# Top-2 expert layers: the inner rows made in turned form, with stationary weights that VectorE picks

## The reference, cut to what matters

```python
# third layer (x: 6250 x 256, layer-normalised first)
logits = xf @ gate_w + gate_b
probs = softmax(logits); top2_vals, top2_idx = top_k(probs, 2)
h = gelu(xf @ w1 + bb1)          # exact gelu, for each expert
y = h @ w2 + bb2
out = sum over the two chosen experts of weight * y
# fourth layer: the same, with a weight of 1 for each of the two
```

## Time and profile before

| | us |
|---|---|
| median of 3 runs (8054.05 to 8055.25) | 8055.03 |
| profiled execution: span from first to last instruction | 9107.5 |
| profiled execution: what lies around the span | not listed |
| expert stage of the third layer: first matmul to first second-layer matmul | 12.15 |
| the same stage: from there to the end of the last second-layer matmul | 424.46 |
| expert stage of the fourth layer, same two parts | 12.02, 424.12 |

### The profile page before, as it was taken

How to read it: one execution, slowest core, us unless ns; L and a number is a source line. 1 busy time by engine, 2 the same in 40 slices (tenths; PEclk the granted TensorE clock), 3 DMA queues, 4 the chain that set the end, 5 groups by cost and what they waited for, 6 DMA issues and landing times. The chain is left out here.

```text
span 9107.5 us, 91729 instructions
## 1 busy us (share of the span) xinstructions
PE 5351.0 (59%) x20514; PEld 4012.4 (44%) x20515; DVE 3669.3 (40%) x8808; ACT 3376.1 (37%) x8020; POOL 4734.0 (52%) x4927
## 2 busy tenths in 40 slices
PE   3789555555534444789433335456556466566796
PEld 2656333444423333656433333344445344445564
DVE  7544555555710000544300001455455455455644
ACT  2522233333333333445333333233334233333553
POOL 5113455555466666034366664666564666664143
PEclk8689776777767776789555555677677767777698
DMA  1421333333233333211201111333332333332213
GB/s 56 178 74 61 91 92 91 86 88 91 67 94 92 92 91 92 84 54 63 79 22 23 23 23 32 94 88 92 87 91 71 95 93 91 88 88 77 94 63 124
DMA packets 395135, 723.41 MB, mean 79 GB/s; under 512 B 117204, under 2 KB 252470, under 8 KB 391602
## 3 DMA queue, kind: packets, MB, share of 16 engines
q0 software_dynamic: 210544, 509.17, 20.1%
q1 hardware_dynamic: 177622, 201.65, 6.9%
q10 hardware_dynamic: 6508, 8.01, 0.2%
HBM read 600.76 MB, written 123.53 MB: 80 GB/s over the span
## 5 line engine op out<-in xcount | busy, mean ns | idle before, releaser
L952 POOL DMA_INDIRECT g_rows<-table,src_idx x2352 | 2244.2, 954 | 1407.4 <-issue 669.9
L1227 PE MATMUL g_p_win<-g_rows,g_hot 128*128 128x264 f32 (+1 forms) x4704 | 1555.7, 490 | 42.5 <-issue 36.0
L1227 PEld LDWEIGHTS g_p_win<-g_rows,g_hot 128*128 128x128 f32 x4704 | 1105.9, 246 | 309.8 <-issue 72.3
L1117 ACT ACTIVATE g_hot<-iota,near 128x128 f32<-128x128 f32 x2352 | 721.4, 387 | 1199.0 <-DMA r_gb<-in_L_ffn_gate_b_dram 873.0
L952 POOL DMA_INDIRECT g2p_rows<-rows,src_idx x784 | 749.3, 956 | 370.4 <-issue 227.7
L952 POOL DMA_INDIRECT gcnp_rows<-table,src_idx x784 | 748.2, 954 | 368.6 <-issue 228.8
L1033 DVE TENSOR_TENSOR g_rows<-g_rows,g_p_w 128x1792 f32<-128x1792 f32 x336 | 679.0, 2021 | 51.1 <-issue 21.2
L1241 PE MATMUL g_p_f<-ones 1*128 1x4 f32 (+1 forms) x336 | 85.9, 324 | 863.9 <-issue 414.1
L1189 PE MATMUL gcnp_p_out<-gcnp_win,gcnp_moved 128*128 128x64 f32 x224 | 62.0, 432 | 732.4 <-ACT gcnp_win L1151 629.7
L1040 DVE TENSOR_TENSOR agg<-agg,g2p_p_out 128x256 f32 x112 | 42.1, 418 | 1102.6 <-PE g2p_p_out L1189 454.1
L1241 PEld LDWEIGHTS g_p_f<-ones 1*128 1x128 f32 x336 | 72.0, 265 | 931.5 <-issue 931.5
(11 more groups left out here) (832 smaller groups left out, 11533.3 us busy)
## 6 DMA issues: line engine op xcount, KB each, us to landing
g_rows<-table,src_idx POOLq DMA_INDIRECT x2352
back<-agg SPq DMA_DIRECT2D x7, 1792.0 KB, 35.0
g_inj<-inject SPq DMA_DIRECT2D x56, 224.0 KB
g2p_rows<-rows,src_idx POOLq DMA_INDIRECT x784
rows<-r_row SPq DMA_DIRECT2D x98, 128.0 KB
gcn_row_in<-back SPq DMA_DIRECT2D x14, 896.0 KB
gcnp_rows<-table,src_idx POOLq DMA_INDIRECT x784
c_row<-back SPq DMA_DIRECT2D x14, 896.0 KB, 13.3
```

The costliest lines, as they stand in the source:

```text
L952: gp.indirect_dma_start(rows[:, s, j, 0:width + H], None, table, bass.IndirectOffsetOnAxis(g.src_idx[:, at:at + 1], 0)).then_inc(got[s], 16)
L1117: last = nc.scalar.activation(hot[:, j, :], g.iota[:, :], ACT.Square, scale=-1.0, bias=g.near[:, bass.ds(c * J + j, 1)])
L1227: last = nc.tensor.matmul(p_win[:, 0:W], hot[:, j, :], rows[:, s, j, :], start=(j == 0), stop=(j == J - 1))
```

## The change

The stationary and the moving operand of the first layer change places. W1 of the tile's expert is stationary, in blocks of 128 inner features, and the turned rows are moving, 128 columns; the result has inner features on the partitions, which is the form that the second layer takes. `turn_hidden` and `copy_hidden` go. b1 then is one number per partition: it is loaded as 32 rows of 128, turned once by PE, copied by VectorE, and given to the gelu as its bias, one gelu for each of the four blocks. The stationary operand has a fixed address in the code, so VectorE copies the expert's W1 into one of two buffers (`pick`). The copy of the turned x moves from ScalarE to VectorE. ScalarE now loads expert numbers too. The eight broadcast loads of b1 are replaced by one load.

```diff
     def load(self, eng, placed):
+        eng.dma_start(self.b1r[:, :], self.b1.rearrange("e (b p) -> (e b) p", p=P)).then_inc(self.b_in, 16)
         for e in range(E):
...
-            eng.dma_start(self.b1s[:, e, :], self.b1[one, :].to_broadcast([P, F])).then_inc(self.w_in, 16)
...
             def _(pe):
+                pe.wait_ge(wt.b_in, 16)
+                nc.tensor.transpose(p_b[:, :], wt.b1r[:, :], g.ident[0:E * HB, 0:E * HB]).then_inc(b_turned, 1)
...
                 def first(i, s, at):
                     pe.wait_ge(copied, i + 3)
-                    pe.wait_ge(biased, i + 1)
-                    for k in range(2):
-                        last = nc.tensor.matmul(p_h[s % 2][:, :], xt[:, s % 2, k, :], w1s[:, of(at), k * F:(k + 1) * F].rearrange("p a f -> p (a f)"), start=(k == 0), stop=(k == 1))
+                    pe.wait_ge(picked, i + 1)
+                    pe.wait_ge(curved, i + 1)
+                    for b in range(HB):
+                        for k in range(2):
+                            last = nc.tensor.matmul(p_h[s % 2][:, b, :], w1c[:, s % 2, k * F + b * P:k * F + (b + 1) * P], xt[:, s % 2, k, :], start=(k == 0), stop=(k == 1))
                     last.then_inc(up, 1)
-                def turn_hidden(i, s, at):
...
                 def second(i, s, at):
-                    pe.wait_ge(h_copied, i + 3)
+                    pe.wait_ge(curved, i + 3)
                     pe.wait_ge(made, i + 1)
...
-                pipeline(pe, TILES, [(2, turn), (1, first), (0, turn_hidden), (-1, second)], AHEAD, before=before)
+                pipeline(pe, TILES, [(2, turn), (1, first), (0, second)], AHEAD, before=before)
...
                 def curve(i, s, at):
-                    ac.wait_ge(biased, i + 3)
-                    ac.wait_ge(h_turned, i + 1)
-                    nc.scalar.activation(hg[:, s, :], hb[:, s, :], ACT.Gelu).then_inc(curved, 1)
-                pipeline(ac, TILES, [(2, copy), (1, curve)])
+                    ac.wait_ge(up, i + 3)
+                    ac.wait_ge(down, i + 1)
+                    for b in range(HB):
+                        last = nc.scalar.activation(ht[:, s % 2, b, :], p_h[s % 2][:, b, :], ACT.Gelu, bias=b1t[:, of(at), b:b + 1].rearrange("p a f -> p (a f)"))
+                    last.then_inc(curved, 1)
+                before, of = experts(ac, ACTE)
+                ac.wait_ge(b_ready, 1)
+                pipeline(ac, TILES, [(1, curve)], AHEAD, before=before)
...
+                dv.wait_ge(b_turned, 1)
+                nc.vector.tensor_copy(b1t[:, :, :].rearrange("p e b -> p (e b)"), p_b[:, :]).then_inc(b_ready, 1)
...
                 dv.wait_ge(b2_in, 16)
...
+                def pick(i, s, at):
+                    dv.wait_ge(up, i + 1)
+                    nc.vector.tensor_copy(w1c[:, s % 2, :], w1s[:, of(at), :].rearrange("p a f -> p (a f)")).then_inc(picked, 1)
+
+                def copy(i, s, at):
+                    dv.wait_ge(turned, i + 3)
+                    dv.wait_ge(up, i + 1)
+                    nc.vector.tensor_copy(xt[:, s % 2, :, :], p_x[s % 2][:, :, :]).then_inc(copied, 1)
...
-                pipeline(dv, TILES, [(1, bias), (0, copy_hidden), (-1, out)], AHEAD, peeled=AHEAD, before=before)
+                pipeline(dv, TILES, [(2, copy), (2, pick), (0, out)], AHEAD, peeled=AHEAD, before=before)
```

More of the change, by code:

```diff
@@ L2556, in __init__ @@
         self.w1s = spare[:, 0:E * 2 * F].rearrange("p (e k f) -> p e (k f)", e=E, k=2)
-        self.b1s = spare[:, E * 2 * F:E * 3 * F].rearrange("p (e f) -> p e f", e=E)
-        self.w2s = sb("w2s", [P, E, self.HB * D])
-        self.w_in = nc.alloc_semaphore(f"{name}_w_in")
+        self.w2s, self.b1r = sb("w2s", [P, E, self.HB * D]), sb("b1r", [E * self.HB, P])
+        self.w_in, self.b_in = nc.alloc_semaphore(f"{name}_w_in"), nc.alloc_semaphore(f"{name}_b_in")
     def load(self, eng, placed):
         F = self.F
+        eng.dma_start(self.b1r[:, :], self.b1.rearrange("e (b p) -> (e b) p", p=P)).then_inc(self.b_in, 16)
         for e in range(E):
@@ L2822, in experts_by_tile @@
     F, HB = wt.F, wt.HB
[L2823 removed]
+    w1s, w2s, w_in = wt.w1s, wt.w2s, wt.w_in
     with Phase(nc, name) as ph:
[L2825 removed]
+        ph.sems += [w_in, wt.b_in]
         b2s, b2_in = ph.sb("b2s", [P, E, D]), ph.sem("b2_in")
@@ L2828, in experts_by_tile @@
         xt = ph.sb("xt", [P, 2, 2, P])
-        hb, hg, ht = ph.sb("hb", [P, 2, F]), ph.sb("hg", [P, 2, F]), ph.sb("ht", [P, 2, HB, P])
+        ht, b1t = ph.sb("ht", [P, 2, HB, P]), ph.sb("b1t", [P, E, HB])
+        w1c = ph.sb("w1c", [P, 2, 2 * F])
         y = ph.sb("y", [P, AHEAD, D])
         p_x = [ph.ps(f"p_x{s}", [P, 2, P]) for s in range(2)]
-        p_h = [ph.ps(f"p_h{s}", [P, F]) for s in range(2)]
-        p_t = [ph.ps(f"p_t{s}", [P, HB, P]) for s in range(2)]
+        p_h = [ph.ps(f"p_h{s}", [P, HB, P]) for s in range(2)]
+        p_b = ph.ps("p_b", [P, E * HB])
         p_y = [ph.ps(f"p_y{s}", [P, D]) for s in range(2)]
-        turned, copied, up, biased, curved, h_turned, h_copied, down, made = (
-            ph.sem(n) for n in ("turned", "copied", "up", "biased", "curved", "h_turned", "h_copied", "down", "made"))
+        b_turned, b_ready, picked, turned, copied, up, curved, down, made = (
+            ph.sem(n) for n in ("b_turned", "b_ready", "picked", "turned", "copied", "up", "curved", "down", "made"))
         x_in = [ph.sem(f"x_in{s}") for s in range(AHEAD)]
@@ L2846, in before @@
                 eng.nop(nofuse=True)
-                loaded[:] = registers(nc, engine, g.tile_expert[0:1, bass.ds(t + AHEAD - 1, steps + 2)], E - 1, waited=False)
-            return before, lambda place: bass.ds(loaded[place + 1], 1)
+                loaded[:] = registers(nc, engine, g.tile_expert[0:1, bass.ds(t + AHEAD, steps + 2)], E - 1, waited=False)
+            return before, lambda place: bass.ds(loaded[place], 1)
         with nc.Block() as block:
@@ L2876, in _ @@
             def _(pe):
-                for s in (turned, up, h_turned, down):
+                pe.wait_ge(wt.b_in, 16)
+                nc.tensor.transpose(p_b[:, :], wt.b1r[:, :], g.ident[0:E * HB, 0:E * HB]).then_inc(b_turned, 1)
+                for s in (turned, up, down):
                     nc.tensor.sem_inc(s, 2)
@@ L2889, in first, with second @@
                     pe.wait_ge(copied, i + 3)
-                    pe.wait_ge(biased, i + 1)
-                    for k in range(2):
-                        last = nc.tensor.matmul(p_h[s % 2][:, :], xt[:, s % 2, k, :], w1s[:, of(at), k * F:(k + 1) * F].rearrange("p a f -> p (a f)"), start=(k == 0), stop=(k == 1))
+                    pe.wait_ge(picked, i + 1)
[3 more added lines that the diff above has]
+                            last = nc.tensor.matmul(p_h[s % 2][:, b, :], w1c[:, s % 2, k * F + b * P:k * F + (b + 1) * P], xt[:, s % 2, k, :], start=(k == 0), stop=(k == 1))
                     last.then_inc(up, 1)
-                def turn_hidden(i, s, at):
+                def second(i, s, at):
                     pe.wait_ge(curved, i + 3)
[L2897 to L2902, removed]
-                    pe.wait_ge(h_copied, i + 3)
                     pe.wait_ge(made, i + 1)
@@ L2907, in second @@
                     last.then_inc(down, 1)
-                pe.wait_ge(w_in, 48 * E)
-                pipeline(pe, TILES, [(2, turn), (1, first), (0, turn_hidden), (-1, second)], AHEAD, before=before)
+                pe.wait_ge(w_in, 32 * E)
+                pipeline(pe, TILES, [(2, turn), (1, first), (0, second)], AHEAD, before=before)
             @block.scalar
             def _(ac):
-                nc.scalar.sem_inc(copied, 2)
                 nc.scalar.sem_inc(curved, 2)
[L2916 to L2919, removed]
@@ L2927, in _ @@
+                    last.then_inc(curved, 1)
+                before, of = experts(ac, ACTE)
+                ac.wait_ge(b_ready, 1)
+                pipeline(ac, TILES, [(1, curve)], AHEAD, before=before)
             @block.vector
             def _(dv):
-                for s in (biased, h_copied, made):
+                for s in (copied, made):
                     nc.vector.sem_inc(s, 2)
-                dv.wait_ge(w_in, 48 * E)
+                dv.wait_ge(b_turned, 1)
+                nc.vector.tensor_copy(b1t[:, :, :].rearrange("p e b -> p (e b)"), p_b[:, :]).then_inc(b_ready, 1)
@@ L2932, in _ @@
+                dv.wait_ge(w_in, 32 * E)
                 dv.wait_ge(b2_in, 16)
                 before, of = experts(dv, DVE)
[L2935 to L2938, removed]
+                def pick(i, s, at):
+                    dv.wait_ge(up, i + 1)
+                    nc.vector.tensor_copy(w1c[:, s % 2, :], w1s[:, of(at), :].rearrange("p a f -> p (a f)")).then_inc(picked, 1)
```

4 lines of the change are left out of this document (removed).

## The result

The changed kernel takes 7973.57 us (median of four runs, 7969.21 to 7978.09); the kernel before, run between them, 8054.54 us (8053.87 to 8055.25). That is 81.0 us less, a ratio of 0.990 with a 95% interval of 0.9886 to 0.9914. The forecast was 7976.0 us, 79 us less.

What follows compares the result with a forecast made beforehand. PE's work per tile was taken to bound the expert stages. Saving 36.6 us per stage plus 3 us at its start, twice, gave -79 us: 8055.03 - 79 = 7976 us, range 7950 to 8035.

Steps and rivals of the forecast that it cites:

- The frame: Both expert stages: microseconds saved there come off the 8055.03 us median at full value; the profiled span is no frame.
- the sum of 79: Whole kernel: 36.6 us less per expert stage plus 3 us less at its start, twice, -79 us.
- First layer and inner turns: PE per tile: 16 matmuls at 0.1116 us make 1.79 us instead of 1.72; dropping the inner turns saves 0.44.
- Sum per tile: PE's work per tile: 0.22 + 1.79 + 1.73 = 3.74 us against 4.11; stage 36.6 us less, 387.9 us.
- ScalarE: Per tile: four gelus taken as 1.5 us, with expert-number loads about 1.8 us, inside the 3.74 us tile.
- VectorE: Per tile: pick 0.69 us, x copy and output addition 0.43 each; sum 1.55 to 2.05 of 3.74 us.
- POOL: Per tile: unchanged, two issues of 1.0 us and 0.3 between; its waiting shrinks from 1.8 to 1.4 us.
- Rival C: POOL becomes the bound, pick and issues excluding each other: 4.9 us per tile, +170 us, 8225 us; chance 0.04.
- Start: Start of each expert stage: second layer begins near 3926.7 instead of 3930.21; bounds -4 to +2, taken as -3 us.
- A: New PE waits, likely at the loop's head, eat 20 to 60 us of the gain: 7992 to 8039; chance 0.14.
- D: No change: a loop through VectorE's in-order queue (copy, pick, output) keeps the tile at 4.1 us; chance 0.04.
- B: First layer's weight loads not hidden: each short matmul pays its own, tile 5.45 us, +275, 8330 us; chance 0.04.

## Why the prediction was right, point by point

*The frame.* Taking the saving from the stages and putting it on the median at full value held. By the traces the stages gave 36.35 and 36.01 us and their starts 3.67 and 3.82 (the fourth layer's start was 12.02 us before and is 8.20), in sum 79.9; the runs gave 81.0. The 1.1 us between are within the scatter of the medians. That the sum of 79 came so close is in part luck: the stages gave 0.8 us less than the forecast, the starts 1.5 us more.

*First layer and inner turns.* 16 x 0.1116 = 1.79 us forecast, 1.79 measured, with a pitch of (1.95 - 0.275) / 15 = 0.1117 us. The row that carried the forecast had the very shape, and was worth more than a rate times columns (1.71) or a load's recorded time (3.04). Inner turns -0.44: shown by putting them back.

*Sum per tile.* 3.74 forecast, 3.73 measured; the stage 387.9 against 388.1.

*ScalarE.* The sum of some 1.8 us was right for partly wrong reasons. Four gelus take 1.14 us and not 1.5, since they start 0.257 us apart though each is recorded with 0.369. The Trainium skill ("ScalarE: Activation LUTs", What ACT_TABLE_LOAD costs) says that activations back to back overlap by some 93 ns; here it is 0.11 us. On the other side the table load did not go with the copy, as I had written, but stayed once in four tiles (0.32 per tile; before, it had been 37 loads for 73 tiles and not one per tile), and the expert numbers cost this queue 1.55 us, not 0.82 (0.39 per tile). All of it had cover.

*VectorE.* The pick took 0.683 us at the median and 0.746 in the mean for 0.69 forecast; the slope of half a nanosecond, which no row had shown, came out as (0.683 - 0.285) / 768 = 0.52 ns against the 256-column copy. The copy took 0.42 and the output 0.43. The cover was there, but the reserve I named (done some 1.8 us later, wanted 3.9 us later) is that of three tiles in four. At the loop's head it is 1 us, as the extra picks showed.

*POOL.* 1.4 us of waiting per tile forecast, 112.4 / 80 = 1.4 measured. Rival C did not come, and the reason given against it, that one pick can hold at most one issue, was not put to the test: picks and issues ran side by side, each a little slower, even with three picks. The two issues with their gaps take 2.6 to 2.7 us, as rival C had it; the 2.3 of the run with half of the layers was too small.

*Start.* From the first turn, the steps forecast put the first first-layer pass at 1.8 us, its end at 5.4 and the second layer at 8.6; measured 1.85, 5.40 and 8.48. So the term was -3.5 by its own working, which I had rounded to -3; it is -3.7 and -3.8. What the forecast left unused: matmuls in PE's idle 5 us ahead of the first rows and a gelu ahead of the tiles shorten the third layer's start by 2.3 to 2.7 us more in the traces.

*Rivals.* A and D: no idle time on PE, and added PE work came out in full. B: refuted at 128 columns by the pitch of 0.1117 us. At 64 columns half of each load shows, 0.056 of the 0.110 us; load and matmul one after the other would have made 0.163. D's queue had about 1 us to spare in its worst tile.

## What to carry to other kernels

PE busy for a whole window suggests that PE bounds it; a cheap proof is to add a known piece of work to the engine and see whether its whole price comes out, then to add some to the neighbours and see how much they take before it does. Price a new instruction by a row of its own shape, and where none exists find out what runs beside it: here a short matmul cost the longer of its columns and the weight load beside it. Take the reserve of an engine from its worst tile in the loop, not from the mean.

## What the runs showed of the hardware that was not expected

- A fp32 matmul of 64 columns with its own weights of 128 columns starts no sooner after the last than one of 128: 0.110 and 0.1117 us; with 8 columns it is 0.111.
- Loading the expert numbers takes 1.554 us on ScalarE's queue and 0.809 to 0.818 us on VectorE's and PE's.
- One gelu ahead of the loop took away a table load of 1.28 us in every pass of the loop, 26.7 us of ScalarE in 300 us, at no change in the rest. Why it had been there was not tried.
- A pick and a POOL issue that overlap each become slower, and neither stops the other: in the kernel with three picks the copies reach 0.83 to 0.95 us for 0.68, and the gather beside them 1.06 for 0.98. The Trainium skill ("SBUF — State Buffer", Who interferes with whom) has the second wait for the whole of the first, if the copy is in a two-port mode; the trace does not name the mode, but if these copies are in it, it disagrees, with a gather of 1.06 us that began 0.73 us into 1.54 us of two such copies and ran beside the second.
- The granted clock in the first pass of the third layer's stage was 0.50 (1.2 GHz) where PE had idled for 5.12 us ahead of the turns before it, and 1.00 (2.4 GHz) where it had been given matmuls in that time, although 0.94 us of idle time lay between the turns and the pass.
